# Cross attention on one core: raw Wo loaded in slot 2, another order in the drain, two of the last four tiles projected whole at the end

## The chip, the core and the metric

One NeuronCore of a Trainium2 chip runs the whole kernel. Its engines are TensorE (PE: matmuls, with weight loads as PEld), VectorE (DVE), ScalarE (ACT), GpSimd (POOL) and SyncE (SP), which here only issues DMAs; ACT issues DMAs as well. Each engine works through its own instruction list in order, and the lists meet at semaphores. The metric is the device time of one execution in microseconds (us); lower is better.

## The reference

```
Q = x @ Wq + bq;  K = c @ Wk + bk;  V = c @ Wv + bv      x: (16, 512, 512), c: (16, 77, 512)
16 heads of 32:  p = softmax(Q K^T / sqrt(32));  ctx = p V
out = ctx @ Wo + bo
result = layer_norm(out + x) * ln_gamma + ln_beta         over the last axis, eps 1e-5
```

All is float32. The kernel keeps that precision by splitting each operand of the big matmuls into a high part (rounded to the matmul's format, ACT) and a low part (the rest, POOL or DVE), and adding three products: high by high, high by low, low by high. So one projection of a 128-row tile over four chunks of 128 is 12 matmuls of 512 columns.

## The kernel before

`project_context` first makes K for all batches and the first two tiles of V. `attend` then runs 64 slots, one for each chunk of four heads: slot n belongs to batch n // 4, chunk n % 4. Every engine has its own `slot(g)`, and `run` writes it out for g = 0 to 67 (66 on some engines), so the order is a hand-written one with fixed lags: in slot g the PE projects Q for chunk g (`project_q`), takes the scores of chunk g - 3 (`scores`), every second slot the products with V of the chunks g - 5 and g - 4 with the sums of the softmax (`values_of_pair`), and projects output tile g - 8 (`project_out`, one chunk of its 12 matmuls between other work). DVE does the row maxima, the low part of Q, the sums over keys (`sum_keys`), their inverse (`invert_sums`), its spread over the rows (`spread`), the product (`divide`, into `cxt`), and adds the residual to an output tile (`add_residual`, which frees the one output bank `p_o` for the next tile and adds up the rows). ACT does the exponentials, the high parts (`ctx_high` makes `ch`), the squares and the normalisation, and issues some DMAs. POOL makes the low parts (`ctx_low` makes `cl`), adds bo to the residual's rows (`add_bo`, in `xn`), takes the inverse standard deviation, and multiplies by gamma and adds beta.

Wo is loaded raw into four tiles that the attention needs soon after (`cxt` twice, `rden`, `vb`), split on ACT (`woh`) and POOL (`wol`), two chunks in each of the slots in `WO_SLOTS`; SP issues its four DMAs in the slot before the first of these. `divide` and `spread` wait for `wo_low`. The scores of a pair of chunks need `z`: 8 DMAs from `qh`, 4 from `ql`, and 4 small ones with the row maxima (`load_maxima`, from `nmt`), issued by SP in that order.

From slot 64 on no Q is left: this is the drain. Slots 64 to 67 each hold two scores, the products with V of one chunk (`values`), tile g - 8 (`project_out`), with the chunk's `sums` between its second and third step, two more scores, and then `project_last` for the last batch, whose four tiles have banks of their own (`last_banks`: `p_q`, `p_a0`, `p_a1`, `p_s0`). `project_last(c)` needs `ch` and `cl` of chunk c of the last batch. After slot 67 comes `project_last(3)`, and then the layer norm of the last tiles: DVE runs a written list of passes (`add_last`, `center_scale`, `divide_shift`), in which `add_last(3)` comes before all `center_scale` of the last tiles, ACT and POOL do the rest, and SP stores.

## Time and profile before

| | |
|---|---|
| median of 3 runs | 606.83 us (604.17 to 607.12) |
| the profiled execution: device time, span of its instructions | 606.88 us, 605.0 us |
| busy: PE, DVE, ACT, POOL | 586.3, 476.1, 402.1, 445.9 us |
| one pair of slots in the steady part (slot 7 and 8, 93.68 to 109.94) | 16.26 us |
| the drain on PE | 557.82 to 595.45 us |

A row of the timeline gives the start, the duration, the engine and the line of the kernel, what is written and read, and in square brackets the idle time of the engine before it and who ended it. `ACTq` and `SPq` are DMA issues of ACT and SP: while an issue runs, the later instructions of that engine's list are not started. "issue" as a releaser means that no other engine's work shown in the profile ended the wait.

### The profile page before, as it was taken

The numbers are of one execution on the slowest core, as the hardware profiler recorded it, in microseconds if no ns is written. First come the engines' busy times: TensorE is split into PE (matmuls) and PEld (weight loads), VectorE is DVE, ScalarE is ACT, GpSimd is POOL, SyncE is SP. The second block draws the span as 40 slices with busy tenths as digits, with TensorE's granted clock in tenths as the row PEclk, the third lists the DMA queues.
The fourth block names the chain that finished last, engine by engine and source line by source line (L and its number), as shares of the span: only waits on it lengthen the run. The fifth ranks groups of instructions, "written<-read, shape, count | busy, mean of one in ns | idle before, by whom it ended". The sixth has DMA issues, their size and how long they took to land.

```text
span 605.0 us, 10107 instructions
## 1 busy us (share of the span) xinstructions
PE 586.3 (97%) x3102; PEld 426.8 (71%) x3102; DVE 476.1 (79%) x775; ACT 402.1 (66%) x837; POOL 445.9 (74%) x396
## 2 busy tenths in 40 slices
PE   8999989999999999999999999999999999999793
PEld 5877856777777777777777777777777777776462
DVE  5535568888888888888888888888888888888676
ACT  5622444577777777777777777777777777667462
POOL 1364253468888888888888898888888888798785
PEclk9999999999999999999999999999999999999898
DMA  7958996989898888989888889889988989896513
GB/s 272 356 206 226 228 241 173 252 195 228 213 226 218 212 222 219 229 213 235 224 211 216 223 215 222 218 211 228 213 226 222 221 224 225 216 226 156 131 56 136
DMA packets 93476, 129.83 MB, mean 215 GB/s; under 512 B 50000, under 2 KB 50000, under 8 KB 93424
## 3 DMA queue, kind: packets, MB, share of 16 engines
q1 hardware_dynamic: 73888, 93.27, 62.0%
q10 hardware_dynamic: 19536, 35.92, 21.5%
q8 instruction: 25, 0.41, 0.3%
q14 instruction: 27, 0.22, 0.1%
HBM read 53.94 MB, written 24.35 MB: 129 GB/s over the span
## 4 chain that ended last, share of the span: by engine, by line
PE 92%; POOL 3%; ACT 1%; DVE 1%; issue 1%; DMA 1%; ACTq 1%; DVEq 0%; SPq 0%; POOLq 0%
PE p_q L642 28%; PE p_o L730 28%; PE p_s L680 10%; PE p_v L691 10%; PE p_a L666 6%; PE pk L323 5%; PE p_o L113 3%; PE pvv L113 1%; DMA cx<-in_ctx_t 1%; PE p_a L747 1%; POOL prob L1189 1%; PE p_q L747 0%; POOL xl L1195 0%; POOL wol L1256 0%; ACTq L857 0%
## 5 line engine op out<-in xcount | busy, mean ns | idle before, releaser
L803 ACT ACTIVATE prob<-p_s 77x512 f32<-77x512 f32 x256 | 142.0, 591 | 77.0 <-PE p_s L680 70.9
L1064 DVE TENSOR_REDUCE nm<-p_a 128x4 f32<-128x308 f32 x256 | 117.9, 469 | 53.8 <-PE p_a L666 50.3
L1195 POOL TENSOR_TENSOR xl<-xt,xh 128x512 fp32r<-128x512 f32 x60 | 77.3, 1290 | 97.6 <-ACT xh L810 97.5
L1005 DVE TRANSPOSE_TENSOR_REDUCE part<-prob 96x64 f32<-96x2048 f32 x64 | 146.7, 2292 | 0.2 <-ACT prob L803 0.2
L642 PE MATMUL p_q<-xl,wqh 128*128 128x512 f32 x256 | 101.1, 395 | 0.0
L642 PE MATMUL p_q<-xh,wqh 128*128 128x512 f32 x256 | 101.1, 395 | 0.0
L642 PE MATMUL p_q<-xh,wql 128*128 128x512 f32 x256 | 101.0, 394 | 0.0
L730 PE MATMUL p_o<-woh,ch 128*128 128x512 f32 x240 | 96.4, 402 | 1.5 <-DVE y L997 1.2
L680 PE MATMUL p_s<-z,ks 97*77 97x512 f32 x256 | 93.1, 403 | 3.3 <-ACT prob L803 1.7
L730 PE MATMUL p_o<-wol,ch 128*128 128x512 f32 x240 | 95.4, 398 | 0.0
L730 PE MATMUL p_o<-woh,cl 128*128 128x512 f32 x240 | 95.2, 397 | 0.0
L818 ACT ACTIVATE qh<-p_q,bq_col 128x512 fp32r<-128x512 f32 x64 | 44.0, 688 | 76.2 <-PE p_q L642 76.2
L1216 POOL TENSOR_TENSOR cl<-cxt,ch 128x512 fp32r<-128x512 f32 x64 | 82.4, 1303 | 14.4 <-ACT ch L828 14.4
L1223 POOL TENSOR_TENSOR xn<-xn,bo_row 128x512 f32<-128x512 f32 x60 | 77.6, 1293 | 4.1 <-DMA bo_row<-in_bo 2.3
L666 PE MATMUL p_a<-kb,qh 128*128 128x308 f32 x256 | 78.4, 306 | 0.7 <-ACT qh L818 0.3
L1211 POOL TENSOR_TENSOR y<-y,beta_row 128x512 f32<-128x512 f32 x58 | 75.6, 1304 | 4.5
L1207 POOL TENSOR_TENSOR y<-y,gamma_row 128x512 f32<-128x512 f32 x58 | 75.3, 1299 | 0.0
L1056 DVE SCALAR_TENSOR_TENSOR ql<-p_q,bq_col,qh 128x512 fp32r<-128x512 f32 x64 | 47.7, 745 | 33.0 <-ACT qh L818 33.0
L691 PE MATMUL p_v<-prob,vb 77*32 77x512 f32 x512 | 62.0, 599 | 0.0
L666 PEld LDWEIGHTS p_a<-kb,qh 128*128 128x128 f32 x256 | 48.4, 189 | 16.0 <-ACT qh L818 1.3
L730 PEld LDWEIGHTS p_o<-woh,ch 128*128 128x128 f32 x240 | 45.5, 190 | 18.2 <-DVE y L997 3.1
L642 PEld LDWEIGHTS p_q<-xh,wql 128*128 128x128 f32 x256 | 48.1, 188 | 11.5
(140 smaller groups left out, 946.6 us busy)
## 6 DMA issues: line engine op xcount, KB each, us to landing
z<-qh SPq DMA_DIRECT2D x256, 128.0 KB, 3.1
z<-ql SPq DMA_DIRECT2D x120, 128.0 KB, 4.2
xn<-in_x ACTq DMA_DIRECT2D x60, 256.0 KB, 3.7
out_dram<-y SPq DMA_DIRECT2D x60, 256.0 KB, 4.2
xt<-in_x_t ACTq DMA_DIRECT2D x58, 256.0 KB, 4.5
ks<-k_high SPq DMA_DIRECT2D x32, 154.0 KB, 4.5
cx<-in_ctx_t SPq DMA_DIRECT2D x4, 616.0 KB, 5.6
k_high<-kth SPq DMA_DIRECT2D x4, 616.0 KB, 3.6
```

The source lines that it names most:

```text
L642: last = nc.tensor.matmul(p_q[:], w[:, kc, P * c:P * (c + 1)], x[:, i, kc, :], start=(kc == 0 and n == 0), stop=(kc == KC - 1 and n == 2))
L666: nc.tensor.matmul(p_a[t % 2][:, 0:HC * S2], qh[:, g.k // 2 % 2, g.k % 2, P * t:P * (t + 1)], kb[g.k // NCH % 2][:, g.k % NCH, :], start=T ...
L680: nc.tensor.matmul(p_s[j % 2][0:S2, :], ks[0:KR, g.k // NCH % 2, h, :], z[0:KR, i, j, g.k % 2, :], start=True, stop=True).then_inc(s_summe ...
L691: nc.tensor.matmul(bank[DK * j:DK * (j + 1), :], vb[0:S2, g.k // NCH % 2, DK * h:DK * (h + 1)], prob[0:S2, g.k % 2, j, :], start=True, sto ...
L730: last = nc.tensor.matmul(p_o[:], x[:, i, kc, P * t:P * (t + 1)], w[:, kc, :], start=(kc == 0 and n == 0), stop=(kc == KC - 1 and n == 2))
L803: nc.scalar.activation(prob[0:S2, g.k % 2, j, :], p_s[j % 2][0:S2, :], ACT.Exp, scale=SCALE).then_inc(prob_ready, 1)
L1005: nc.vector.tensor_reduce(part[:, g.k % 2, :], prob[0:KP, g.k % 2, :, :].rearrange("p h (i r) -> p (h i) r", r=DK), AX_X, ALU.add, apply_t ...
L1064: nc.vector.tensor_reduce(nm[:, t, g.k % 2:HALF:2], p_a[t % 2][:, 0:HC * S2].rearrange("p (h k) -> p h k", k=S2), AX_X, ALU.max, negate=Tr ...
L1195: nc.gpsimd.tensor_tensor(xl[:, i, n.k % KC, :], xt[:, n.k % 2, :], xh[:, i, n.k % KC, :].bitcast(F32), ALU.subtract).then_inc(xl_ready, 1)
L1211: nc.gpsimd.tensor_tensor(rows(m), rows(m), beta[:], ALU.add).then_inc(y_done, 1)
L1216: nc.gpsimd.tensor_tensor(cl[:, i, g.k % NCH, :], cx[:, g.k % 2, :], ch[:, i, g.k % NCH, :].bitcast(F32), ALU.subtract).then_inc(cl_ready, 1)
L1223: nc.gpsimd.tensor_tensor(xn[:, m.k % 2, :], xn[:, m.k % 2, :], bo[:], ALU.add).then_inc(xb_ready, 1)
```

## The change

1. `WO_SLOTS` goes from (4, 5) to (3, 4): SP issues the raw Wo in slot 2 instead of 3, and ACT and POOL split it one slot earlier.
2. Slot 63: the four DMA issues of ACT that copy `ql` into `z` (`copy_low`) move from the end of the slot to two places between the exponentials, two issues at each; SP stores tile 52 ahead of the maxima; ACT's load of the last tile's rows into `vb` moves from slot 63 to slot 65, and POOL's `add_bo_last(3)` from slot 64 to slot 66.
3. Drain, PE: `sums` goes behind the whole of `project_out` and the scores; `values` uses two banks in turn, and the sums of a chunk go into the bank that the chunk does not use.
4. Drain, DVE: `add_residual` of tile g - 8 stands between `sum_keys` and `invert_sums` of the same slot, instead of at the start of the next one. After slot 66 it is the same with tile 59.
5. Drain, ACT and POOL: `ctx_high` of chunk 59 goes behind two exponentials and a square; `add_bo` goes ahead of `ctx_low` and of gamma and beta.
6. `project_last(c)` for c < 3 does two tiles instead of three (four for c = 2), and `project_last(3)` does one chunk of tiles 0 and 1 and all four chunks of tiles 2 and 3.

SP's list of DMAs at slots 2 to 4, before (`z<-nmt` are the maxima):

```order
L526 DMA kb1<-k_high 32x4x77 [waits kb1_zeroed]
L526 DMA kb1<-k_high 32x4x77 x3
L580 DMA z<-qh 32x1024 [waits qh_ready]
L580 DMA z<-qh 32x1024 x7
L580 DMA z<-ql 32x1024 [waits ql_ready]
L580 DMA z<-ql 32x1024 x3
L567 DMA cxt<-in_Wo 128x512
L567 DMA rden<-in_Wo 128x512
L567 DMA vb<-in_Wo 128x512
L567 DMA cxt<-in_Wo 128x512
L575 DMA z<-nmt 1x32x32 [waits max_turned]
L575 DMA z<-nmt 1x32x32 x3
```

and in the changed kernel, where the four loads of Wo stand ahead of the copies of `qh`:

```order
L526 DMA kb1<-k_high 32x4x77 [waits kb1_zeroed]
L526 DMA kb1<-k_high 32x4x77 x3
L567 DMA cxt<-in_Wo 128x512
L567 DMA rden<-in_Wo 128x512
L567 DMA vb<-in_Wo 128x512
L567 DMA cxt<-in_Wo 128x512
L580 DMA z<-qh 32x1024 [waits qh_ready]
L580 DMA z<-qh 32x1024 x7
L580 DMA z<-ql 32x1024 [waits ql_ready]
L580 DMA z<-ql 32x1024 x3
L575 DMA z<-nmt 1x32x32 [waits max_turned]
L575 DMA z<-nmt 1x32x32 x3
```

ACT's list at the end of slot 63 and the start of 64, before (`L857` is `copy_low`, `L877` the load of the last tile, the second `CAST` is `ch` of chunk 59):

```order
L828 CAST ch<-cxt 128x512 [waits cx_ready]
L848 ACTIVATE over_d<-rstd 128x1 [waits rstd_ready]
L850 ACTIVATE nmr<-ysum,over_d 128x1 [waits over_d_ready]
L882 ACTIVATE y<-y,nmr,rstd 128x512 [waits nmr_ready]
L857 DMA z<-ql 32x1024 [waits ql_ready]
L857 DMA z<-ql 32x1024 x3
L877 DMA vb<-in_x 128x512 [waits pv_summed]
L828 CAST ch<-cxt 128x512 [waits cx_ready]
L803 ACTIVATE prob<-p_s0 77x512 [waits part_ready,pv_summed,s_summed]
L803 ACTIVATE prob<-p_s1 77x512 [waits s_summed]
L834 ACTIVATE xn,ssd<-y,ysum 128x512 [waits y_ready]
L863 DMA xn<-in_x 128x512 [waits squared]
```

and now from the second exponential of the slot's last pair on (`L859` is `copy_low`; two more of its issues stand further up, behind the first pair of exponentials):

```order
L805 ACTIVATE prob<-p_s1 77x512 [waits s_summed]
L859 DMA z<-ql 32x1024 [waits ql_ready]
L859 DMA z<-ql 32x1024
L830 CAST ch<-cxt 128x512 [waits cx_ready]
L850 ACTIVATE over_d<-rstd 128x1 [waits rstd_ready]
L852 ACTIVATE nmr<-ysum,over_d 128x1 [waits over_d_ready]
L884 ACTIVATE y<-y,nmr,rstd 128x512 [waits nmr_ready]
L805 ACTIVATE prob<-p_s0 77x512 [waits part_ready,pv_summed,s_summed]
L805 ACTIVATE prob<-p_s1 77x512 [waits s_summed]
L836 ACTIVATE xn,ssd<-y,ysum 128x512 [waits y_ready]
L865 DMA xn<-in_x 128x512 [waits squared]
L830 CAST ch<-cxt 128x512 [waits cx_ready]
```

The copies now stand ahead of `ch` of chunk 58 and the normalisation instead of behind them, and `ch` of chunk 59 (the last row) comes two exponentials, a square and a DMA issue later.

PE's list in slot 67, from the last sums (`p_v`) on, before:

```order
L713 MATMUL p_v1<-part,sel 32x16 [waits rec_ready,cx_ready,part_ready]
L713 MATMUL p_v1<-part,sel 32x16 x3
L730 MATMUL p_o<-woh,ch 128x512
L730 MATMUL p_o<-wol,ch 128x512
L730 MATMUL p_o<-woh,cl 128x512
L730 MATMUL p_o<-woh,ch 128x512
L730 MATMUL p_o<-wol,ch 128x512
L730 MATMUL p_o<-woh,cl 128x512
L747 MATMUL p_q<-woh,ch 128x512 [waits cl_ready,ch_ready]
L747 MATMUL p_q<-wol,ch 128x512
L747 MATMUL p_q<-woh,cl 128x512
L747 MATMUL p_a0<-woh,ch 128x512
```

and now:

```order
L714 MATMUL p_v0<-part,sel 32x16 [waits cx_ready,part_ready]
L714 MATMUL p_v0<-part,sel 32x16 x3
L748 MATMUL p_q<-woh,ch 128x512 [waits cl_ready,ch_ready]
L748 MATMUL p_q<-wol,ch 128x512
L748 MATMUL p_q<-woh,cl 128x512
L748 MATMUL p_a0<-woh,ch 128x512
L748 MATMUL p_a0<-wol,ch 128x512
L748 MATMUL p_a0<-woh,cl 128x512
L748 MATMUL p_q<-woh,ch 128x512 [waits cl_ready,ch_ready]
L748 MATMUL p_q<-wol,ch 128x512
L748 MATMUL p_q<-woh,cl 128x512
```

Before, the sums were followed by 6 matmuls of tile 59 and 18 of chunk 2 ahead of the first matmul that needs chunk 3. Now the 6 of tile 59 lie ahead of the sums, and 6 matmuls of chunk 2 follow; the second `p_q` row that waits is the first that needs chunk 3. Behind it stand 30 matmuls instead of 12.

```diff
--- before.py
+++ after.py
...
 LAG_STORE = 11
-WO_SLOTS = (4, 5)
+WO_SLOTS = (3, 4)
 ROWS_SLOT = 8
...
-        gamma_tail, beta_tail = p_s[1], p_v[1]
+        gamma_tail, beta_tail = p_s[1], p_v[0]
         x_last = [xt[:, 0, :], xt[:, 1, :], bv_row[:], vb[:, B % 2, :]]
...
         den_pair = p_a[0][:, HC * S2:HC * S2 + 2 * QB]
-        den_single = p_v[1][:, 0:QB]
+        den_single = [p_v[1 - k][:, 0:QB] for k in range(2)]
...
                     if at_edge(g):
+                        if not g.back(1).is_first():
+                            store(g.back(LAG_STORE))
                         load_maxima(c)
...
                         load_z(2, i, ql)
-                if g.back(LAG_STORE).valid(NS):
+                if g.back(LAG_STORE).valid(NS) and not at_edge(g):
                     store(g.back(LAG_STORE))
...
                     pe.wait_ge(vb_in[g.k // NCH % 2], g.over(PAIR, 1, 16))
-                bank = p_v[0] if single(g) else p_v[g.k % 2]
+                bank = p_v[g.k % 2]
                 for j in range(HC):
...
                 pe.wait_ge(part_ready, g.over(1, 1))
-                pe.wait_ge(cx_ready, NG - LAG_PV)
-                at_least(pe, rec_ready, g.over(1))
+                pe.wait_ge(cx_ready, g.over(1))
                 for j in range(HC):
-                    last = nc.tensor.matmul(den_single[DK * j:DK * (j + 1), :], sel[:], part[:, g.k % 2, QB * j:QB * (j + 1)],
+                    last = nc.tensor.matmul(den_single[g.k % 2][DK * j:DK * (j + 1), :], sel[:], part[:, g.k % 2, QB * j:QB * (j + 1)],
                                             start=True, stop=True)
...
                 pe.wait_ge(cl_ready, NG - NCH + c + 1)
-                steps = [(t, c) for t in range(QT - 1)]
-                if c >= NCH - 2:
-                    steps += [(QT - 1, kc) for kc in (range(NCH - 1) if c == NCH - 2 else (c,))]
+                steps = [(t, c) for t in range(QT // 2)]
+                if c == NCH - 1:
+                    steps += [(t, kc) for t in range(QT // 2, QT) for kc in range(NCH)]
                 for t, kc in steps:
...
                 if not g.valid(NG):
-                    pe.wait_ge(cx_ready, v.over(1, -1) if v.over(1) == NG - LAG_PV else v.over(1))
+                    pe.wait_ge(cx_ready, v.over(1, -1))
+                    pe.wait_ge(rec_ready, v.over(1))
                     values(v)
                 for kc in range(KC):
-                    if kc == 2 and not g.valid(NG):
-                        sums(v)
                     if o.valid(NS):
...
                         rowmax_scores(g, kc)
+                if not g.valid(NG):
+                    sums(v)
                 c = last_batch_chunk(g, LAG_PV + 1)
...
-            def copy_low(g):
+            def copy_low(g, heads):
...
                 act.wait_ge(ql_ready, PAIR * g.u + g.k + 1)
-                for j in range(HC):
+                for j in heads:
                     act.dma_start(z[DK * 2:DK * 3, i, j, :, :].bitcast(F32),
...
                 if g.back(1).is_first():
-                    copy_low(g)
-                if g.k % 2 == 0 and w.valid(NG) and not single(w):
+                    copy_low(g, range(HC))
+                if g.k % 2 == 0 and w.valid(NG) and not single(w) and g.valid(NG):
                     ctx_high(w)
...
                     exp(s, 1)
+                if at_edge(g) and not g.back(1).is_first():
+                    copy_low(g, range(HC // 2))
                 if m.valid(NS):
...
                     load_residual(g.back(LAG_NORM - 2))
+                if g.k % 2 == 0 and w.valid(NG) and not single(w) and not g.valid(NG):
+                    ctx_high(w)
                 if s.valid(NG):
...
                     exp(s, 3)
+                if at_edge(g) and not g.back(1).is_first():
+                    copy_low(g, range(HC // 2, HC))
                 if g.k % 2 == 1 and w.valid(NG) and not single(w):
...
                     split_x_high(Slot(0, KC))
-                if at_edge(g) and not g.back(1).is_first():
-                    copy_low(g)
                 if n.valid(NG):
...
                     load_last(t)
-                if last_tile(g.back(-1)) == 0:
+                if last_tile(g) == 1:
                     load_last(QT - 1)
...
                 if single(g):
-                    nc.vector.reciprocal(rec[:, g.k % 2, :], den_single).then_inc(rec_ready, 1)
+                    nc.vector.reciprocal(rec[:, g.k % 2, :], den_single[g.k % 2]).then_inc(rec_ready, 1)
                 else:
...
                 at_least(dve, cl_ready, g.over(1, -1))
-                nc.vector.tensor_tensor(cx[:, g.k % 2, :], p_v[0 if single(g) else g.k % 2][:], rden[:], ALU.mult).then_inc(cx_ready, 1)
+                nc.vector.tensor_tensor(cx[:, g.k % 2, :], p_v[g.k % 2][:], rden[:], ALU.mult).then_inc(cx_ready, 1)
...
                     add_bv(i)
-                if m.valid(NS) and not g.valid(NG):
+                if last_tile(g) == 0:
                     add_residual(m)
...
                     q_low(g)
+                if not g.valid(NG):
+                    add_residual(g.back(LAG_OUT))
                 if v.valid(NG) and single(v):
...
-            add_residual(Slot(0, NS - 2))
             sum_keys(Slot(0, NG - 1))
             minus_mean_over_std(Slot(0, NS - 3))
+            add_residual(Slot(0, NS - 1))
             invert_sums(Slot(0, NG - 1))
...
             variance_of_squares(Slot(0, NS - 2))
-            add_residual(Slot(0, NS - 1))
             center_scale(NS - 2, 0)
...
                     ctx_low(e)
+                if b.valid(NS) and not g.valid(NG):
+                    add_bo(b)
                 if g.k % 2 == 0 and w.valid(NG) and not single(w):
...
                     shift(g.back(LAG_SCALE))
-                if b.valid(NS):
+                if b.valid(NS) and g.valid(NG):
                     add_bo(b)
...
                     add_bo_last(t)
-                if last_tile(g) == 0:
+                if last_tile(g) == 2:
                     add_bo_last(QT - 1)
...
```

## Rows read from the trace of the kernel before

**Rows 1.** The page: chain of work that ended last, shares of the span by engine.
```profile
PE 92%; POOL 3%; ACT 1%; DVE 1%; issue 1%; DMA 1%; ACTq 1%; DVEq 0%; SPq 0%; POOLq 0%
```
**Rows 2.** Timeline, PE: first projection matmul of slots 5 to 9 (start, us, engine).
```profile
74.19 0.39 PE L642 MATMUL p_q<-xh,wqh 128*128 128x512 f32 x1
...
84.68 0.40 PE L642 MATMUL p_q<-xh,wqh 128*128 128x512 f32 x1
...
93.68 0.39 PE L642 MATMUL p_q<-xh,wqh 128*128 128x512 f32 x1
...
102.84 0.40 PE L642 MATMUL p_q<-xh,wqh 128*128 128x512 f32 x1
...
109.94 0.39 PE L642 MATMUL p_q<-xh,wqh 128*128 128x512 f32 x1
```
**Rows 3.** Timeline, PE: idle time in slots 5 and 6, and its releaser in brackets.
```profile
80.35 0.67 PE L680 MATMUL p_s<-z,ks 97*77 97x512 f32 x2 [1.28 <-issue]
...
91.34 0.46 PE L680 MATMUL p_s<-z,ks 97*77 97x512 f32 x1 [1.70 <-ACT prob L803]
```
**Rows 4.** Timeline, SyncE's queue of DMA issues around the raw Wo.
```profile
63.75 5.54 SPq L580 DMA_DIRECT2D z<-qh  x8
...
71.88 0.59 SPq L567 DMA_DIRECT2D cxt<-in_Wo  x1
...
73.95 2.95 SPq L575 DMA_DIRECT2D z<-nmt  x4
```
**Rows 5.** Line L567 (raw Wo): time from issue to landing.
```profile
DMA to landing us min/median/max: 4.1/5.3/6.8
```
**Rows 6.** Stretches: busy time of each engine, PE clock, DMA share, GB/s.
```profile
62.00:63.00 1.00, 1.00 (x6) 0.77 (x5) 0.00 (x0) 0.00 (x0) 0.22 (x1) 1.00 0.75 213
```
**Rows 7.** Timeline, DVE in slot 6: the second product of the first pair.
```profile
89.45 0.69 DVE L1049 TENSOR_TENSOR cxt<-p_v,rden 128x512 f32<-128x512 f32 x1 [2.56 <-POOL wol L1256]
```
**Rows 8.** Timeline, ACT and its DMA issues at the end of slot 63.
```profile
557.53 0.61 ACT L828 CAST ch<-cxt 128x512 fp32r<-128x512 f32 x1
...
558.61 2.82 ACTq L857 DMA_DIRECT2D z<-ql  x4
...
562.53 0.62 ACT L828 CAST ch<-cxt 128x512 fp32r<-128x512 f32 x1 [3.11 <-issue]
```
**Rows 9.** Timeline, PE in slots 64 and 65: its idle time.
```profile
563.06 0.26 PE L713 MATMUL p_v<-part,sel 96*32 96x16 f32 x8 [1.89 <-DVE part L1005]
...
569.21 0.60 PE L730 MATMUL p_o<-woh,ch 128*128 128x512 f32 x1 [1.23 <-DVE y L997]
```
**Rows 10.** Stretch after the second of them, columns as in rows 6.
```profile
569.43:572.60 3.17, 3.17 (x15) 2.08 (x15) 2.36 (x4) 0.58 (x2) 3.16 (x4) 0.51 0.22 83
```
**Rows 11.** Timeline, the last sums, last chunk's products, and last tile's first DVE pass.
```profile
586.60 0.26 PE L713 MATMUL p_v<-part,sel 96*32 96x16 f32 x8
...
592.49 0.40 PE L747 MATMUL p_q<-woh,ch 128*128 128x512 f32 x1
...
596.43 0.68 DVE L1127 SCALAR_TENSOR_TENSOR vb<-p_s,vb 128x512 f32<-128x512 f32 x1
```
**Rows 12.** Groups by line, 557 to 596 us: count, busy, mean ns, idle before.
```profile
L1216 POOL TENSOR_TENSOR cl<-cxt,ch 128x512 fp32r<-128x512 f32 x6 | 7.8, 1296 | 7.1 <-ACT ch L828 7.1
L803 ACT ACTIVATE prob<-p_s 77x512 f32<-77x512 f32 x13 | 7.4, 589 | 8.0 <-PE p_s L680 7.5 <-ACT xn L834 0.4
...
L1223 POOL TENSOR_TENSOR xn<-xn,bo_row 128x512 f32<-128x512 f32 x4 | 5.2, 1291 | 0.0
...
L828 ACT CAST ch<-cxt 128x512 fp32r<-128x512 f32 x6 | 3.7, 611 | 4.0 <-issue 3.1 <-DVE cxt L1049 0.9
L834 ACT ACTIVATE xn<-y,ysum 128x512 f32<-128x512 f32 x5 | 3.6, 720 | 0.6 <-DVE y L997 0.5
...
L1023 DVE STREAM_TRANSPOSE rden<-rec 128x512 f32<-128x512 f32 x5 | 3.6, 711 | 0.1
...
L997 DVE SCALAR_TENSOR_TENSOR y<-p_o,xn 128x512 f32<-128x512 f32 x5 | 3.4, 682 | 4.6 <-POOL xn L1223 3.3 <-PE p_o L730 1.3
```

## The prediction

> **What bounds the kernel now.** I read the page's chain first, since it says which engine's time counts: PE holds 92% of it [rows 1]. So only idle or slowed time of PE, and what follows its last matmul, can be won or lost. The timeline of PE then shows where that is. The even part is the same slot after slot and no edit touches it. What is left lies at two ends.
>
> The start: slot 5 (with products with V, like every odd slot) lasts 84.68 - 74.19 = 10.49 us, where slot 7 takes 102.84 - 93.68 = 9.16; slot 6 lasts 9.00, where slot 8 takes 109.94 - 102.84 = 7.10 [rows 2]. So 1.33 and 1.90 us too much, and each has an idle stretch of PE of that kind inside: 1.28 us before the scores of chunk 2 and 1.70 us before a score in slot 6 [rows 3].
>
> The drain: PE idles 1.89 us for the sums' input in slot 64 and 1.23 us for the output bank in slot 65 [rows 9], and right after it runs at a granted clock of 0.51 for 3.2 us, that is on the lower level, 1.2 GHz [rows 10]. The end: after the last sums (586.60) PE still has matmuls enough until the last chunk's products start at 592.49 [rows 11].
>
> **The change part by part, start.** The 1.70 us hang on DVE's product, which waited 2.56 us for the low part of Wo on POOL [rows 7]; ACT's high part and then the exponentials queue behind it. With the split one slot (about 9 us) earlier this wait is gone for certain: -1.90. Next in line behind it are the scores and exponentials in their steady order, which in slots 7 and 8 let PE run without a gap.
>
> The 1.28 us are a DMA wait. SP issued the maxima of the pair from 73.95 on, behind the four Wo loads from 71.88 on [rows 4], which took 4.1 to 6.8 us to land [rows 5]: one issued near 73.5 lands at about 80.3, and the scores start at 80.35. In the new order Wo is issued at about 62.7, after SP's loads of kb, while SP waits for `qh` anyway until 63.75. Four issues take 73.95 - 71.88 = 2.07 us, so the copies of `z` start at 64.8 instead of 63.75, and the maxima are issued 2.07 - 1.05 = 1.0 us earlier, by 75.8. The bytes of Wo still lie ahead of them; but between 62 and 63 us the engines for DMA are busy 0.75 of the time [rows 6], so there is room. I take the wait as gone: -1.33; the other bound is nothing gained here. ACT now waits for Wo at the end of slot 3: issued at 62.7 and 63.2, landing 4.1 to 6.8 us later [rows 5], two casts of 0.61 us, done between 68.5 and 71.2, and its next work is at about 70.1. I take 0; at the late end 1.1 us are lost. Start: -3.23, bounds -0.8 and -3.23.
>
> In the Trainium skill, DMA: Bandwidth & Descriptors, section "Issuing engines are not separate DMA queues", all issues share the same 16 engines and interleave. By that rule a load moved ahead is paid by what follows it, and the gain of 1.33 would be only what the idle share allows (an estimate by that page: 0 to 1.33). The landing of Wo right at the start of the scores agrees with it.
>
> **Drain, slots 63 and 64** (times on the axis of before, start not yet taken off; durations [rows 12]; a square with its accumulator is 0.81 us, an inverse of std 0.55, a reciprocal 0.26, a product 0.69 in the same view). The four copies of `ql` hold up ACT's list for 2.82 us [rows 8], four issues of 0.70. Before, they stood behind all of slot 63's work and, with one more load, made `ch` of chunk 59 late (562.53, after 3.11 us of idle ACT). Now two of them come before the square (from 554.5) and two behind the last exponential (from 557.65). So `ch` of 58 moves from 557.53 to about 559.15, the normalisation ends at 561.05, and the exponentials of chunk 61 start at 561.0 instead of 563.05. But `ch` of 59 now stands behind two exponentials, a square and a DMA issue: 561.0 + 1.07 + 0.81 + 0.33 = 563.2, later than 562.53. Its `cl` takes POOL 1.3 us more: 565.2. PE no longer waits for the sums; it reaches the fourth step of tile 56 at 562.2 and waits there for `cl` of 59 until 565.2: one idle stretch of 3.0 us where 1.89 and some tenths were. The fourth step ran at 564.67 before.
>
> **Slots 65 and 66.** From 565.2 on: fourth step 0.70, score 0.24, sums 0.2. The bank of tile 56 is emptied in the same slot, since bo was added ahead of the low parts; the 1.23 us of [rows 9] are gone. The products with V of 61 wait for its last exponential and run 567.25 to 568.25, tile 57 from 568.3 at full clock, where before it began at 569.21 at half. From there PE has per slot 4 scores, 1.0 of products with V, 2.8 of tile, 0.2 of sums and 1.4 of two last tiles, 6.4 us. A second ring has the same length: `cl` 1.30, inverse 0.55, `add_bo` 1.29, residual 0.77, reciprocal 0.26, spread 0.71, product 0.69, `ch` 0.61, 6.2 us. Products with V of 63 start at 579.65, before at 584.01: 4.36 earlier, of which 1.4 (slots 65 and 66 have three matmuls less each, six by 0.233) is work put off to the end.
>
> **Slot 67 and the end.** Tile 59 ends at 583.5, sums and chunk 2's six matmuls at 585.1. Now the list on POOL decides: `cl` of 62 from 581.65 to 582.95, inverse 583.5, the last tile's bo (moved here) 584.75, bo of tile 59 586.0. The residual of 59 stands before the reciprocal of 63 on DVE: 586.8; reciprocal 587.05, spread 587.8, product 588.5, `ch` 589.15, and behind gamma, beta and an inverse on POOL `cl` of 63 at 590.6. PE idles 585.1 to 590.65, 5.5 us, where before it idled nowhere; then it has 30 matmuls, spaced 0.233 us, 7.0 us. The last tile's first DVE pass starts at 590.65 + 7.0 + 0.25 = 597.9, before at 596.43 [rows 11]. What follows it is unchanged, 605.0 - 596.43 = 8.57 us, since DVE's list keeps all last passes behind this one. So +1.47 at full clock.
>
> The clock: the low stretch of before cost 3.2 us x (1 - 0.233/0.43) = 1.5 us, and came after idle time of about 4 us in all within eight [rows 9, 10]. After 5.5 us of idle time I take one such stretch: +1.5. For the 3.0 us in slot 64 I take another: fourth step, score and sums cost 0.8 more before the ring of POOL and DVE goes on: +0.8. Bounds 0 and, with 30 matmuls all at 0.43, +5.9 for the first, 0 and 1.5 for the second.
>
> **The sum.** Span 605.0 - 3.23 + 1.47 + 1.5 + 0.8 = 605.5; the profiled execution took 606.88 for a span of 605.0, so 1.9 more: 607.4 us. The median of the runs, 606.83, is the profiled time within 0.1. What a measurement of this kernel tells from no change is 0.5%, 3.0 us; the forecast is no change, a gain at the start given back at the end.
>
> **Rivals.**
> - ACT's issues hide. If the copies of slot 63 run beside the exponentials and do not hold up the square, `ch` of 59 follows the sums' product by 561 and the 3.0 us in slot 64 shrink to 0.5. All later is 2.3 us earlier, with no lower clock there: 607.4 - 2.3 - 0.8 = 604.3, and 602.8 if the last wait costs no clock. For it: ACT waited 1.6 us for scores in slot 63. Against: in [rows 8] ACT did nothing during the issues. Chance 0.26.
> - The clock holds at the end. 5.5 us of idle time without a lower stretch: 607.4 - 1.5 - 0.8 = 605.1. For it: the idle stretches of 1.28 and 1.70 us at the start cost no clock. Chance 0.12.
> - The change doesn't do what it says at the start: maxima still late, as the DMA engines are full: 607.4 + 1.33 = 608.7. Chance 0.10.
> - Slower: PE stays on the lower level through the last 30 matmuls. All at 0.43 instead of 0.233 cost 5.9 instead of 1.5: 611.8. It turns slower than 609.9 once 13 matmuls more than the 7 or 8 of one low stretch run low. Against: the stretch of [rows 10] ended after 3.2 us of busy PE. Chance 0.12.
> - In the Trainium skill, TensorE: Matmul & The Clock Gate, section "What's actually happening", the lower level is the default and activity lifts it. By that rule the long run of matmuls lifts it again and this rival is cut short; the row's 3.2 us agree.
>
> **How the numbers follow.** Forecast 0.40, rivals as given. Faster than 603.8: 0.17 of the first rival's 0.26, which lies on both sides of that bound, and 0.05 of the second's, where the last wait is shorter too: 0.22. Slower than 609.9: the fourth rival's 0.12, and 0.03 of the third's with both clock losses at their ends: 0.15. Same: 0.63. The range goes from 602.8 (first rival) to 610.3 (forecast with the late Wo and a longer low stretch); the forecast's own range is 605 to 609.5.
>
> **What would show it.** Slots 5 and 6 at 9.2 and 7.1 us, no idle time before DVE's product in slot 6. PE idle about 3 us before the fourth step of tile 56, released by `cl`. No wait of PE for the sums or for the bank. PE idle about 5 us before the last chunk's products, released by `cl` of 63 on POOL, then 30 matmuls, the first seven or so at half clock. It is wrong if that last wait is under 3 us, or if slot 5 keeps its excess.

## The result

The changed kernel is slower: 611.91 us median of 20 runs against 607.63 us for the kernel before (20 runs, taken in turn with them), ratio 1.0072, 95% interval 1.0053 to 1.0091. That is +4.3 us by the medians; forecast were 607.4 us and a range of 602.8 to 610.3. One of the 20 runs of the changed kernel took 970.94 us, at a mean granted clock of 0.554, and the ratio leaves it out. The profiled execution took 613.67 us for a span of 611.8.

I compare three stretches that split a profile without a remainder: up to the start of slot 7 on PE, from there to the last tile's first DVE pass, and the tail behind that.

| stretch | before | after | difference | forecast |
|---|---|---|---|---|
| to the start of slot 7 | 93.68 | 95.31 | +1.63 | -3.23 |
| slot 7 to the last tile's first pass | 502.75 | 507.89 | +5.14 | +3.77 |
| tail | 8.57 | 8.60 | +0.03 | 0 |
| span | 605.0 | 611.8 | +6.8 | +0.5 |

### The profile page after: what moved, and what is told of

Same layout as the page of the kernel before. It is cut to its first block, busy times and chain, and to the rows that moved or that the text cites. A ratio compares the mean times of both kernels' runs of the same rounds, so it can differ in the third digit from the quotient of the medians.

```text
span 611.8 us, 10108 instructions
## 1 busy us (share of the span) xinstructions
PE 590.9 (97%) x3102; PEld 429.6 (70%) x3102; DVE 476.2 (78%) x775; ACT 402.2 (66%) x837; POOL 446.0 (73%) x396
## 4 chain that ended last, share of the span: by engine, by line
PE 88%; SPq 3%; POOL 3%; issue 1%; ACT 1%; DMA 1%; DVE 1%; ACTq 0%; DVEq 0%; POOLq 0%
PE p_o L731 26%; PE p_q L644 26%; PE p_s L682 10%; PE p_v L693 9%; PE p_a L668 5%; PE pk L323 5%; SPq L580 2%; PE p_o L113 2%; DMA z<-ql 1%; PE pvv L113 1%; PE pk L331 1%; PE p_a L748 1%; SPq L575 1%; POOL cl L1223 1%; POOL prob L1196 1%
```

## The profile after

The start, PE's timeline (start, duration, tiles, in brackets the idle time before and what ended it). The first row is the start of slot 5, the third that of slot 6, the fourth that of slot 7; it answers [rows 2, 3].

```profile
74.07 0.39 PE L644 MATMUL p_q<-xh,wqh 128*128 128x512 f32 x1
...
82.32 0.86 PE L682 MATMUL p_s<-z,ks 97*77 97x512 f32 x2 [3.38 <-issue]
...
88.21 0.40 PE L644 MATMUL p_q<-xh,wqh 128*128 128x512 f32 x1
...
95.31 0.39 PE L644 MATMUL p_q<-xh,wqh 128*128 128x512 f32 x1
```

Slot 6 lasts 7.10 us, to the hundredth what was forecast: the wait for the low part of Wo is gone. Slot 5 lasts 14.14 us instead of 10.49. Its wait, which was to vanish, grew from 1.28 to 3.38 us, and PE then ran on the lower level, 1.2 GHz (windows: length, busy PE, granted clock, DMA share, GB/s):

```profile
80.00:82.00 2.00, 0.00 (x0) 1.00 1.30 186
82.00:83.00 1.00, 0.68 (x3) 0.80 1.15 227
83.00:84.00 1.00, 1.00 (x4) 0.50 1.07 209
84.00:85.00 1.00, 1.00 (x5) 0.50 1.06 209
85.00:86.00 1.00, 1.00 (x4) 0.50 1.11 213
```

SP's queue, to be held against [rows 4], shows when the maxima went out: Wo now goes out from 62.66, the twelve issues of the `z` copies behind it take 8.7 us (before 8.1), and `nmt` is issued from 73.34, 0.6 us earlier than before. So the late scores are not a late issue; what took longer is the way from issue to landing.

```profile
62.66 0.42 SPq L567 DMA_DIRECT2D cxt<-in_Wo  x1
...
64.57 6.19 SPq L580 DMA_DIRECT2D z<-qh  x8
70.81 2.49 SPq L580 DMA_DIRECT2D z<-ql  x4
73.34 2.97 SPq L575 DMA_DIRECT2D z<-nmt  x4
```

In the chain of waits one issue among them took 1.38 us where its neighbours took 0.59, and the last copy of `ql` needed 6.81 us to land. PE started 2.8 us behind that. That it waited for the maxima then is inferred from its list, since this trace has no row for their landing.

```profile
67.47 0.59 SPq L580
68.06 0.04 issue
68.10 1.38 SPq L580
...
72.71 6.81 DMA z<-ql
79.52 2.81 issue
82.32 0.86 PE p_s L682 x2
```

From issue to landing the copies of that stretch took 5.1 to 6.8 us, before 2.3 to 4.3:

```profile
DMA to landing us min/median/max: 5.1/5.9/6.8
```

The drain, PE's timeline in slots 64 and 65 and at the end (answers [rows 9, 11]):

```profile
566.41 0.47 PE L731 MATMUL p_o<-woh,ch 128*128 128x512 f32 x1 [2.23 <-POOL cl L1223]
...
569.03 1.94 PE L693 MATMUL p_v<-prob,vb 77*32 77x512 f32 x8
```

```profile
594.38 0.57 PE L748 MATMUL p_q<-woh,ch 128*128 128x512 f32 x1 [4.22 <-POOL cl L1223]
```

Both waits are the two forecast ones, each released by `cl` as said, each shorter than said (3.0 and 5.5). What was not forecast is the clock behind the first (windows as above):

```profile
567.00:568.00 1.00, 1.00 (x12) 0.65 0.00 0
568.00:569.00 1.00, 1.00 (x2) 0.50 0.00 0
...
573.00:574.00 1.00, 1.00 (x3) 0.50 0.08 25
574.00:575.00 1.00, 1.00 (x5) 0.94 0.74 238
```

That is 6.8 us at the lower level (0.70 in the first of these windows, six whole ones, 0.12 in the last), where [rows 10] had 3.2 of such time, and 3.4 counted in the same way. The products with V of 61 take 1.94 us in it instead of 1.07. And the last tile's first pass:

```profile
603.20 0.69 DVE L1135 SCALAR_TENSOR_TENSOR vb<-p_s,vb 128x512 f32<-128x512 f32 x1 [1.92 <-PE p_s L748]
```

## The experiments

All were timed in turn with the kernel before, 5 rounds and 6 to 12 runs each, but for second traces of before and after, which are one run each. Slot 5 and slot 6 are lengths on PE, "rest" is the stretch from slot 7 to the last tile's first pass; these three are from the one profiled execution, medians and ratios from the timed runs. A ratio compares a kernel with the runs of before that were timed with it, whose median lay between 606.03 and 607.63, and it is not the quotient of two medians: for hd_warm, whose runs fall into two groups (606.1 to 607.9 and 610.8 to 612.6), that quotient would be 1.0084.

| kernel | slot 5 | slot 6 | rest | median us | ratio, 95% |
|---|---|---|---|---|---|
| before | 10.49 | 9.00 | 502.75 | 607.63 | |
| before, again | 9.58 | 8.99 | 501.53 | one run | |
| after | 14.14 | 7.10 | 507.89 | 611.91 | 1.0072 (1.0053 to 1.0091) |
| after, again | 11.93 | 7.06 | 507.99 | one run | |
| start_alone | 14.22 | 7.10 | 502.16 | 606.36 | 0.9991 (0.9966 to 1.0015) |
| drain_alone | 12.58 | 8.99 | 507.53 | 611.45 | 1.0080 (1.0054 to 1.0106) |
| wo_act | 10.14 | 7.10 | 502.11 | 603.93 | 0.9959 (0.9937 to 0.9982) |
| halves | 9.18 | 7.10 | 501.34 | 603.08 | 0.9958 (0.9919 to 0.9998) |
| early | 9.16 | 7.06 | 503.03 | 606.31 | 0.9987 (0.9962 to 1.0012) |
| start0 | 9.17 | 7.06 | 502.53 | 606.35 | 0.9984 (0.9961 to 1.0007) |
| hd | 11.83 | 7.09 | 507.52 | 609.90 | 1.0080 (1.0050 to 1.0110) |
| hd_fill | 10.89 | 7.10 | 502.91 | 604.62 | 0.9964 (0.9938 to 0.9991) |
| hd_warm | 15.15 | 7.10 | 505.03 | 611.30 | 1.0048 (1.0014 to 1.0083) |
| hd_copy | 9.17 | 7.05 | 509.06 | 612.92 | 1.0128 (1.0090 to 1.0166) |
| e_old_last | 9.16 | 7.10 | 504.32 | 607.44 | 1.0015 (0.9994 to 1.0036) |
| e_fill_res | 9.16 | 7.06 | 503.06 | 608.07 | 1.0017 (0.9995 to 1.0039) |
| e_fill_warm | 9.16 | 7.06 | 501.44 | 603.73 | 0.9961 (0.9936 to 0.9986) |
| s0_fill_warm | 9.36 | 7.11 | 500.58 | 603.28 | 0.9934 (0.9911 to 0.9957) |
| a_fill | 9.73 | 7.10 | 502.88 | 603.65 | 0.9958 (0.9939 to 0.9977) |
| a_fill_warm | 9.72 | 7.11 | 500.59 | 601.23 | 0.9903 (0.9878 to 0.9928) |

**The two parts apart: start_alone.** The kernel before with one line:

```
-WO_SLOTS = (4, 5)
+WO_SLOTS = (3, 4)
```

> The kernel before with the change's start alone: raw Wo issued in slot 2 ahead of the pair's z copies, split in slots 3 and 4. Theory A (Wo's 1 MB in front of the copies, which are themselves enough to fill the DMA engines, makes the pair's maxima land later): slot 5 lasts about 14.1 us and slot 6 about 7.1, slot 9 starts 1.6 us later than before, so +1.6 us (ratio 1.003); PE idle about 3.4 us before the scores of chunk 2, then a granted clock of 0.5. Rival B (the late start belongs to that one execution or to the drain's other order, and the term I forecast is right): slot 5 lasts 9.2 us, -3.2 us, ratio 0.995.

**drain_alone.** The changed kernel with that line undone.

> The changed kernel with raw Wo issued in slot 3 and split in slots 4 and 5 again, so the drain's part alone. Theory A: the drain costs +5.3 us of span as the trace of after shows against before from slot 63 on (2.2 us idle before the fourth step of tile 56, 4.2 us before the last chunk's products, low clock 6.6 and 3.4 us): ratio 1.007 to 1.009, slots 5 and 6 as before (10.5 and 9.0 us). Rival B (parts interact: the low clock in the drain comes from the phase that the start leaves): +3.8 us or less, ratio at most 1.006, and a low stretch near 3.2 us instead of 6.6.

The parts add: -0.09% and +0.80% make +0.71%, measured 0.72%, each within about 0.25%. So the drain carries the whole loss, with a ratio in theory A's range, and the start, forecast at -3.2 us, is worth nothing that can be measured. Slot 5 of drain_alone was to be as before, 10.5 us, and came at 12.58. The trace of start_alone shows the shape of A (14.22 us, 3.44 us idle), but the interval of its ratio holds neither A's 1.003 nor B's 0.995: a first sign that one trace of slot 5 tells little.

**Bytes or order: wo_act and halves.** In wo_act the load stands in ACT's list instead of SP's (shortened; `WO_SLOTS` is (3, 4) here too):

```
 # SP, end of a slot
-if g.back(WO_SLOTS[0] - 1).is_first():
-    for kc in range(KC):
-        load_wo(kc)          # sp.dma_start
 # ACT, end of a slot
+if g.back(WO_SLOTS[0] - 1).is_first():
+    for kc in range(KC):
+        load_wo(kc)          # act.dma_start
 for kc in wo_in_slot(g):
     split_wo_high(kc)
```

> As the start alone, but the four loads of raw Wo are issued by ACT at the end of slot 2, and so stand in ACT's DMA queue instead of SP's; the z copies and the maxima then have no Wo ahead of them in their own queue. Theory A1 (all queues share the DMA engines, and the bytes are what delays the maxima): PE still idles 3 us or more before the scores of chunk 2 and slot 5 lasts 13 to 14 us, total +1 to +2 us. Theory A2 (order within SP's queue delays them): the maxima land earlier, idle time under 1 us, slot 5 about 9.5 us, total -2 to -3 us. Under either, ACT spends 1.3 us on the issues in slot 2, which can delay qh by no more than that.

In halves two chunks go out in slot 2 and two in slot 3:

```
-if g.back(WO_SLOTS[0] - 1).is_first():
-    for kc in range(KC):
-        load_wo(kc)
+for kc in wo_in_slot(g.back(-1)):
+    load_wo(kc)
```

> The kernel before with raw Wo split in slots 3 and 4 as in the change, but only two chunks of it (0.5 MB) issued in slot 2 ahead of the z copies, and two in slot 3 behind them. Theory A (bytes ahead of the maxima): all four are still ahead of the maxima, so PE's idle time before the scores of chunk 2 lies between that of before (1.3 us) and that of the start alone (3.4 us), about 2.3; total about -0.5 us. Rival (the loads before the copies alone are at fault, since DMA engines run at their limit from then on without a gap): about the same as before in slot 5 (10.5 us) and slot 6 at 7.1: total -1.9 us.

Both are 0.4% faster than before. The trace of wo_act has 0.94 us of idle time before the scores of chunk 2, that of halves none. Neither A1 (3 us) nor the estimate for halves (2.3 us) came in: in these two traces the same megabyte stands ahead of the maxima and does not hold them up. What wo_act gave is near A2's forecast: idle time under 1 us, slot 5 at 10.14 us (9.5 said) and -0.4%, that is -2.5 us. By the Trainium skill, DMA: Bandwidth & Descriptors, section "Issuing engines are not separate DMA queues", the issuing engine should have made no difference beyond the issue time. Whether the runs contradict it is left open by the next ones.

**The same start, five traces: hd and its kin.** hd is the changed kernel with the load by halves; hd_fill, hd_warm and hd_copy differ from it only in the drain, halves differs from it only there too.

> The changed kernel, with raw Wo loaded by halves (two chunks in slot 2, two in slot 3). The start is to be as in the run by halves (no idle before the scores of chunk 2, slot 9 at 105 us where before has 109.9), the drain as in the run of the drain alone. Theory (the two parts simply add): ratio 0.996 + 0.008 = 1.004. Rival (the drain's low clock hangs on what came before it): ratio at 1.000 or below, with a low stretch near slot 65 of 3.2 us instead of 6.6.

Up to slot 6 these five kernels issue the same work in the same order, yet slot 5 lasts 9.18, 11.83, 10.89, 15.15 and 9.17 us (halves, hd, hd_fill, hd_warm, hd_copy; the last four ran on one chip, so another chip does not explain it). PE's rows in hd and in hd_warm:

```profile
80.85 0.65 PE L681 MATMUL p_s<-z,ks 97*77 97x512 f32 x2 [2.61 <-issue]
```

```profile
82.26 1.11 PE L681 MATMUL p_s<-z,ks 97*77 97x512 f32 x2 [3.61 <-issue]
```

Nor is it a fixed property of each program. The 12 timed runs of halves fall into two groups, seven from 601.5 to 603.6 us and five from 607.4 to 611.5; these runs have no rows for slot 5, so that it is the cause of their spread is likely, not shown. The second trace of after had 1.18 us of idle time there and slot 5 at 11.93, that of before 0.37 us and 9.58. The expectation of hd (1.004) failed: 1.008, as if the halves brought nothing.

> The changed kernel once more, for a second look at its slot 5. Theory (the wait for the maxima differs from one execution to the next): slot 5 differs from the 14.1 us of the first look by over 0.5 us, while slot 6 (7.1), the wait in slot 64 (2.2) and the last wait (4.2) repeat within 0.3 us. Rival (14.1 us is what this order gives): 14.0 to 14.3 again.

> The kernel before once more, for a second look at its slots 5 and 6. Theory (the wait for the maxima varies in this order too): slot 5 differs from 10.49 us by over 0.5 us, with slot 6 at 9.0 again and the waits of the drain (1.89 and 1.23 us) within 0.1 us. Rival: 10.4 to 10.6 us.

```profile
79.33 1.05 PE L682 MATMUL p_s<-z,ks 97*77 97x512 f32 x2 [1.18 <-issue]
```

```profile
79.43 0.66 PE L680 MATMUL p_s<-z,ks 97*77 97x512 f32 x2 [0.37 <-issue]
...
90.40 0.46 PE L680 MATMUL p_s<-z,ks 97*77 97x512 f32 x1 [1.69 <-ACT prob L803]
```

For slot 5 both theories held: the wait for that landing is a draw, from nothing to 3.6 us over all traces, while slot 6 repeats, and in after the two waits of the drain do too (2.49 and 4.22 us, in the first trace 2.23 and 4.22). In before one of them did not. The 1.90 us for the sums came again, the 1.23 us for the output bank were gone: this time PE fell to the lower level behind the first wait, in slot 64 (windows with PE alone),

```profile
562.00:564.00 2.00, 1.89 (x13) 0.65 0.99 147
564.00:566.00 2.00, 2.00 (x6) 0.50 0.83 264
```

and so came later to the bank. In the old drain the clock is a draw as well. All seven traces of it have the 1.9 us for the sums. Behind them before again has a low stretch of 3.4 us and wo_act one of 6.8; before, start_alone, early and start0 have 3.4 us of it only behind the wait for the bank (1.0 to 1.26 us), and halves has both waits and no low stretch at all. The rest runs from 501.3 to 503.0 us in these seven traces, so the 502.75 of before is near its upper end.

**Wo far from the copies: early and start0.** early loads Wo ahead of slot 0 (from 44.4 us), start0 as the first thing of SP's list in this stage (the same four lines, ahead of the kb loads; meant for 36 us, in the trace from 40.7).

```
-if g.back(WO_SLOTS[0] - 1).is_first():      # in SP's slot
-    for kc in range(KC):
-        load_wo(kc)
+for kc in range(KC):                        # ahead of run(sp, slot)
+    load_wo(kc)
```

> The kernel before with raw Wo split in slots 3 and 4 as in the change, but all four chunks loaded before slot 0, at about 44 us, where the DMA engines are half idle. Theory (the wait before the scores of chunk 2 is a race between the pair's maxima and PE, which comes out between 0 and 3.6 us from one execution to the next because 1 MB of Wo shares the DMA engines with them; over about 1.8 us it also costs clock): without Wo near them slot 5 lasts 9.2 us in every execution, slot 6 7.1: ratio 0.990 to 0.993 and a narrow spread of the runs, under 3 us from lowest to highest. Rival (the spread is that of the copies and the k loads themselves, with or without Wo): runs still spread over 7 us or more and the ratio is 0.996, as with the halves.

> The kernel before with raw Wo split in slots 3 and 4, and its four loads as the first thing of SP's list in this stage, at about 36 us, ahead of kb. The load ahead of slot 0 (44 us) moved the wait from slot 5 to slot 2 (2.7 to 3.1 us for qh). Theory (1 MB costs nothing only where it lands before the copies of the first pair begin at 50 us): slots 2 to 6 last 6.6, 7.1, 7.1, 9.2 and 7.1 us, slot 7 starts at 89.7, ratio 0.990 to 0.993, runs within 4 us. Rival (whatever is displaced, kb here, comes late in its turn): a new wait of PE of 1 us or more before slot 1, and a ratio of 0.996 or above.

In all six kernels of these two starts slot 5 lasts 9.16 to 9.36 us: without Wo near them the maxima of this pair are late by 0.16 us at most. But the time went elsewhere. early has, for slots 2 and 3,

```profile
59.62 0.41 PE L665 MATMUL p_a<-kb,qh 128*128 128x308 f32 x1 [2.93 <-ACT qh L817]
...
66.59 0.66 PE L679 MATMUL p_s<-z,ks 97*77 97x512 f32 x2 [1.25 <-DMA z<-nmt]
```

since ACT waited 7.36 us for `xt` (row below), and now the maxima of the first pair are late; start0 has 2.23 us for `qh` in slot 1 and a granted clock of 0.5 behind it, and slot 1 lasts 10.20 us instead of 6.7. The ratio of start0 is its rival's. That of early, 0.9987, is above both of its cases, and the spread of its runs, 4.1 us, lies between them. None of the places that were tried from 40 us on was free; they differ in what the megabyte pushes aside.

```profile
57.60 0.62 ACT L809 CAST xh<-xt 128x512 fp32r<-128x512 f32 x1 [7.36 <-DMA xt<-in_x_t]
```

**The last wait: hd_fill, e_old_last, e_fill_res.** hd_fill puts the 18 matmuls that need nothing of the last chunk ahead of the wait:

```
-pe.wait_ge(ch_ready, NG - NCH + c + 1)
-pe.wait_ge(cl_ready, NG - NCH + c + 1)
-steps = [(t, c) for t in range(QT // 2)]
-if c == NCH - 1:
-    steps += [(t, kc) for t in range(QT // 2, QT) for kc in range(NCH)]
-for t, kc in steps:
+late = [(t, kc) for t in range(QT // 2, QT) for kc in range(NCH - 1)] if c == NCH - 1 else []
+steps = late + [(t, c) for t in range(QT if c == NCH - 1 else QT // 2)]
+for n, (t, kc) in enumerate(steps):
+    if n == len(late):
+        pe.wait_ge(ch_ready, NG - NCH + c + 1)
+        pe.wait_ge(cl_ready, NG - NCH + c + 1)
```

> As hd, but PE does the first three chunks of the last two tiles (18 matmuls) before it waits for the last chunk's parts, and only 12 matmuls behind that wait. Theory (the end pays for an idle PE, 4.2 us, and then for the low clock, about 1.5 us): the 18 matmuls fit into the idle time, the last add starts 4.2 + 1.5 = 5.7 us earlier than in hd, ratio 0.9945 to 0.996. Rival 1 (the low clock alone is at fault and comes from the drain as a whole): the gain is 4.2 us, 12 matmuls at half clock cost 1.5 as before. Rival 2 (POOL's list sets the end): the last products start when the low part comes, the same instant in both; what is behind them on DVE queues up instead and the gain is under 3 us.

The rest falls from 507.52 to 502.91, -4.6 us, and the ratio by 0.0116, more than that (start draws are in it). In its timeline the 18 matmuls end 0.2 us ahead of the last chunk's products, all at full clock, 0.233 us from one start to the next:

```profile
590.39 0.40 PE L747 MATMUL p_s<-woh,cl 128*128 128x512 f32 x1
590.83 0.47 PE L747 MATMUL p_q<-woh,ch 128*128 128x512 f32 x1
591.14 0.40 PE L747 MATMUL p_q<-wol,ch 128*128 128x512 f32 x1
```

So the low clock at the end came with the idle time, as the theory said. The gain is 1.1 us short of the theory's 5.7, since rival 2 is right in part: the last product ends near 593.9, but DVE, which ran its passes almost without a gap from 591.80, came to the last tile's first pass only at 594.92. What limits the end there is DVE's list. e_old_last takes the old partition of tiles back (three by chunk) on the new drain; e_fill_res puts the residual of tile 59 behind the last product on DVE.

> The changed kernel with the early load of Wo, and with the last batch's tiles as before the change: three of them projected chunk by chunk, 12 matmuls behind the last wait instead of 30. The time from the start of slot 7 to the last add is 502.1 us in the runs with the drain of before and 507.6 in those with the drain of after. Theory (the idle PE at the end is paid because the work that could fill it stands behind the wait): 503 to 504. Rival (slots 65 to 67 get 1.4 us of PE work more each and that delays the last chunk as much): 506 to 507.

> The changed kernel with the early load of Wo, with 18 of the last 30 matmuls ahead of the last wait, and with the residual of tile 59 behind the last product on DVE instead of ahead of the reciprocal. The run with the 18 matmuls ahead took 502.9 us from the start of slot 7 to the last add. Theory (the residual, which waits 2.3 us for bo on POOL, holds up rec of 63 by 1.9 us): the last low part comes 1.9 us earlier, of which up to 1.5 show, 501.4 to 502.0. Rival (18 matmuls fill PE to the end anyway, or the low part waits for its place in POOL's list): 502.9, no gain.

504.32: near the theory, with 0.71 us of the last wait left. 503.06: the rival, no gain, and for its second reason. POOL ends the low part of 63 498.84 us behind the start of slot 7, in hd_fill 498.68: it stands there behind gamma, beta and an inverse without a gap, so an earlier product does not bring it forward.

**The wait in slot 64: hd_warm, a_fill, e_fill_warm.** Nine products that nothing uses, ahead of the fourth step of tile 56:

```
+if last_tile(g) == 0 and kc == KC - 1:
+    pe.wait_ge(max_ready, NG * QT)
+    for n in range(9):
+        nc.tensor.matmul(p_a[1][:], woh[:, n % KC, 0:P], woh[:, n % KC, :], start=True, stop=True)
```

> As hd, with nine more matmuls (products that nothing uses, into a free bank, 2.1 us) ahead of the fourth step of tile 56, where PE idled 2.2 us for the low part of chunk 59. Theory (that idle time is what costs 6.6 us of low clock, of which some 3 us show at the end): clock 1.0 from the fourth step of tile 56 to the products with V of 61 and beyond, last products 1.5 to 3 us earlier than in hd, ratio lower by 0.003 to 0.005. Rival (the low clock comes from the short matmuls and small waits around it, or the ring over DVE and POOL sets the pace there anyway): no gain, within 0.001 of hd.

```profile
564.16 2.23 PE L780 MATMUL p_a<-woh 128*128 128x512 f32 x9
566.85 0.47 PE L730 MATMUL p_o<-woh,ch 128*128 128x512 f32 x1 [0.46 <-POOL cl L1227]
...
569.09 1.06 PE L692 MATMUL p_v<-prob,vb 77*32 77x512 f32 x8
```

The rest falls by 2.5 us, to 505.03, and the ratio by 0.0032, both as the theory said; the median rises from 609.90 to 611.30, with slot 5 at 15.15 us in the trace and two groups of runs. The granted clock of hd_warm is 1.00 there, that of hd is not; first two stretches of hd, then the same of hd_warm:

```profile
566.00:568.00 2.00, 2.00 (x10) 0.50 0.35 131
568.00:570.00 2.00, 2.00 (x6) 0.50 0.00 0
```

```profile
566.00:568.00 2.00, 1.54 (x11) 1.00 0.30 108
568.00:570.00 2.00, 1.88 (x19) 1.00 0.00 0
```

> The changed kernel with the early load of Wo, with 18 of the last 30 matmuls ahead of the last wait, and with the nine unused products in slot 64's idle time. If the two gains add (4.6 us and 2.5 us in their own runs, from the start of slot 7 to the last add: 507.5 to 502.9 and to 505.0) this stretch takes 500.4 us. Rival (the unused products gave their gain in the last wait, which is gone here): 502.9. With the start without a wait the ratio would be 0.987 to 0.990 in the first case.

> As the kernel with Wo issued by ACT, the 18 matmuls ahead of the last wait and the nine unused products, but without those nine. Theory (the unused products keep the clock up through slot 65 and are worth 2.3 to 2.5 us, whatever stands at the end): PE idles 2.2 to 2.5 us in slot 64, a clock of 0.5 for 6 to 7 us, 502.9 us from slot 7 to the last add, ratio 0.9903 + 0.004 = 0.994. Rival (their gain of 2.5 us was that of single looks): within 0.001 of 0.990.

e_fill_warm reached 501.44, between its two cases, and a ratio of 0.9961 where 0.987 to 0.990 was expected; its start (slot 7 at 90.9 us instead of 89.7) explains a part of that. a_fill took 502.88 and a_fill_warm 500.59, so 2.3 us in the traces, and in the timed runs 0.9958 against 0.9903 (0.0055 or 3.3 us, intervals about 0.002 each way, timed at different times). e_fill_res and e_fill_warm, which were timed side by side and differ by the nine products and the place of one residual, are as far apart: 1.0017 and 0.9961. All nine traces with the new drain and without the nine products have a low stretch of 6.8 us in slots 64 and 65, none of the four with them has one. The nine products pay.

**The copies: hd_copy.** The four copies of `ql` in one piece again:

> As hd, with the four copies of ql in slot 63 in one piece behind all other work of ACT again, as before the change. If ACT's stall on the first two copies (1.3 us before the square) is on the path, the square and ch of 58 come 1.3 us earlier but the copies land later and the scores of chunk 62 follow them: my estimate is 0 to +1 us. If the copies in pieces cost what the prediction charged for them, the wait of PE in slot 64 shrinks from 2.2 to about 1 us and the total falls by 1 to 2 us.

Both guesses were wrong: 509.06, +1.5 us, and a ratio 0.005 higher. In one piece the issues end at 558.49 and ACT's next two exponentials wait for them,

```profile
555.80 2.69 ACTq L858 DMA_DIRECT2D z<-ql  x4
558.61 1.08 ACT L804 ACTIVATE prob<-p_s 77x512 f32<-77x512 f32 x2 [2.00 <-issue]
```

1.6 us later behind slot 7 than in hd, and PE's wait in slot 64 is 3.18 us instead of 2.47. The timed intervals just overlap (1.0050 to 1.0110, 1.0090 to 1.0166), but trace and ratio point the same way: this part of the change is worth its place.

**The best: s0_fill_warm and a_fill_warm.** The changed kernel with the 18 matmuls ahead, the nine products, and Wo first in SP's list, or issued by ACT in slot 2.

> The changed kernel with raw Wo first in SP's list of the stage (36 us), 18 of the last 30 matmuls ahead of the last wait, and the nine unused products in slot 64. Theory: slot 7 at 89.7, the last add 501.4 later at 591.1, and 8.6 behind it: span 599.7, 601.6 us, ratio 0.990 to 0.992, better than before and after. Rival (kb late at the start): 0.995 or above.

> The changed kernel with raw Wo issued by ACT in slot 2, 18 of the last 30 matmuls ahead of the last wait, and the nine unused products in slot 64. By the runs so far: ratio 0.9959 with the old drain, and 502.1 - 501.4 = 0.7 us less from slot 7 to the last add, so 0.995. A rival says that the parts of the start and of the drain do not add: 0.999.

s0_fill_warm came between its two cases, 0.9934, with slot 7 at 93.3 instead of 89.7 (the wait for `qh` in slot 1 again). a_fill_warm did better than both of its: it takes 601.23 us, 1.0% less than the kernel before (interval 0.7 to 1.2%) and so, by the two ratios, 1.7% less than the changed one; its six runs lie within 1.4 us. Its last wait is 0.23 us:

```profile
586.77 0.47 PE L741 MATMUL p_q<-woh,ch 128*128 128x512 f32 x1 [0.23 <-POOL cl L1228]
```

## Why the prediction was wrong, step by step

The median came 4.5 us above the forecast. By the timed runs 2.7 of them are the start (-3.2 forecast, -0.5 by start_alone), 1.1 the drain (+3.8 forecast, +4.9 by drain_alone), and 0.8 the kernel before itself, whose median was 607.63 over 20 runs and not 606.83. The prediction's own sign of being wrong, that slot 5 keeps its excess, came in.

**Start, -1.90 (low part of Wo): right.** Slot 6 is 7.05 to 7.11 us in every kernel with the earlier split, 8.99 or 9.00 in every other.

**Start, -1.33 (maxima): the step that failed.** I wrote "one issued near 73.5 lands at about 80.3", then moved the issue by 1.0 us (it moved by 0.6) and took the wait as gone, on a DMA share of 0.75 in one microsecond. That treated a landing as a constant behind its issue, and it is none: slot 5 in the order of before gave an excess over 9.16 of 1.33 and 0.42 (3.42 in drain_alone, which issues the same there), in the order of after 4.98, 2.77 and (start_alone) 5.06. So 1.33 was one draw, the new order draws from a worse lot, by 2.5 us on the mean of these six traces, and that eats the 1.90; six traces don't settle the size, the timed runs do. The timed start is -0.1%, with an interval of -0.3 to +0.2%; the forecast was -0.5%. The rival "maxima still late, as the DMA engines are full" named this wait and set its price at 1.33, from the far bound "nothing gained": the bound had to reach beyond that, since a megabyte moved ahead of the copies can also make them later. The sentence on the skill's rule (the gain an estimate of 0 to 1.33) has the same fault.

**Slot 64: wait right in kind, clock mis-sized.** Forecast 3.0 us of wait and 0.8 for clock. The wait was 2.23. For the clock: the products with V of 63 start 490.33 us behind slot 7 in before; 4.36 us earlier was forecast at full clock; hd_warm, whose clock stays up, has them at 582.03 - 96.02 = 486.01, that is 4.32 earlier, the forecast to 0.04. after has them at 584.31 - 95.31 = 489.00. So the low stretch costs 3.0 us and not 0.8 (at most 0.3 of it is something else: hd_warm's fourth step already started that much earlier behind slot 7). I had assumed that only the work of slot 64 would be slow; the stretch lasted 6.8 us, over the whole of the products of 61 and most of tile 57, which stand in the ring.

**The end: right in kind, 0.9 us too dear.** From those products to the last pass 19.75 us were forecast (with 1.5 for clock) and 18.89 came: the wait is 4.22 us instead of 5.5. The 30 matmuls took 603.20 - 0.25 - 594.38 = 8.57 us against 7.0 at full clock, 1.57 for clock, forecast 1.5. Together: -0.86 + 3.0 - 0.8 = +1.3 us, the 5.14 against 3.77 of the table. The 3.77 started from one trace of before; against the mean of the seven traces of the old drain, 502.2, the new one, 507.7 in four, costs 5.5.

**The rivals.** "ACT's issues hide": no; ACT stood still for 1.34 us before the square, as forecast. "The clock holds at the end": no. "PE stays on the lower level through the last 30 matmuls" gave 611.8 us, near the median, by the wrong road: about eight of them were slow. By the Trainium skill, TensorE: Matmul & The Clock Gate, section "What's actually happening", activity lifts the level; at the end the row agrees (the clock was back after 3.4 us of busy PE, 594.6 to 598.0), and slot 65 shows that it can take longer: PE was busy there all through the 6.8 us.

**What stays open.** Why the landing of the maxima varies is not settled; no row shows when those of this pair land. With the load issued by ACT (wo_act, a_fill, a_fill_warm: 0.94, 0.53 and 0.52 us idle) it may draw from a better lot than with the load in SP's queue, or have been lucky. The spread of the timed runs favours the former: 4.4 and 3.2 us over 12 runs of wo_act and a_fill, 10.0 and 10.4 over 12 of halves and hd_fill, which have the same drains and load by halves on SP. The ratios of each pair are alike, 0.9959 and 0.9958, 0.9958 and 0.9964. Nor is it settled why the clock falls behind one idle stretch and not behind another of the same length.

## What to carry to other kernels

A wait that ends with a DMA's landing in a crowded stretch is a draw: measure it in several executions before it gets a price, and let its lower bound reach past zero when a large load is moved ahead. Idle time of PE can cost twice, itself and a slow stretch behind it, so put matmuls that need nothing ahead of the wait they would otherwise stand behind (4.6 us here), and in a drain even unused ones can pay (2.3 us). Take the kernel before from several traces too, as its own idle stretches may or may not be followed by slow ones. Price a stretch at the lower clock by the work of the loop that it falls on, not by what follows at once.

## What the runs showed of the hardware

- Idle time alone did not tell whether the clock would fall. What slot 5 lost beyond 9.16 us and its idle time: 0.05 us for 1.28 us idle (before), 0.05 for 1.68 (hd_fill), 0.06 for 2.61 (hd), all with a granted clock of 1.00 throughout; but 1.59 for 1.18 (after, again), 1.59 for 1.83 (drain_alone), 1.60 for 3.38 (after), 2.38 for 3.61 (hd_warm), all with a stretch at 0.50. And in the old drain, behind 1.9 us and mostly 1.0 to 1.26 us more, the low stretch was 0, 3.4 or 6.8 us long.
- A low stretch behind 2.2 us of idle time lasted 6.8 us in slots 64 and 65, twice as long as the one at the end behind 4.2 us (3.4), with PE busy in both.
- A DMA issue on SP that takes 0.59 us took 1.38 us while the DMA engines' share stood at 1.05. It is not the new order's own: in before an issue of `ks`, whose neighbours take 0.44 and 0.49, took 1.37 at a share of 1.08.
